# Result rows of single token tiles added one unit later, and six buffers for the experts' rows

## The reference, cut to what matters

```python
logits = xt @ Wr + br
top_p, top_idx = jax.lax.top_k(softmax(logits), 2)
weights = top_p / top_p.sum(axis=-1, keepdims=True)
xe = xn[None] * ln_g[:, None, :] + ln_b[:, None, :]            # per expert
h = gelu(einsum('end,edh->enh', xe, W1) + b1[:, None, :], approximate=False)
y = einsum('enh,ehd->end', h, W2) + b2[:, None, :]
out = (weights[:, :, None] * y_of_the_two_experts).sum(axis=1)
x = x + out
```

## Time and profile before

| | |
|---|---|
| median of 3 runs | 2281.2 us |
| the profiled execution | 2286.24 us |
| its span, first to last instruction | 2284.5 us |
| mean granted clock of TensorE | 0.953 |
| busy: PE, DVE, ACT, POOL | 89%, 50%, 27%, 46% |
| experts' units in the span | about 1850 to 2284.5 us |
| single tiles | about 2153 to 2284.5 us |

### The profile page before, as it was taken

How to read it: one execution, slowest core, us unless ns; L and a number is a source line. 1 busy time by engine, 2 the same in 40 slices (tenths; PEclk the granted TensorE clock), 3 DMA queues, 4 the chain that set the end, 5 groups by cost and what they waited for, 6 DMA issues and landing times.

```text
span 2284.5 us, 26178 instructions
## 1 busy us (share of the span) xinstructions
PE 2023.8 (89%) x8235; PEld 1382.6 (61%) x8235; DVE 1136.1 (50%) x2348; ACT 606.6 (27%) x1262; POOL 1051.0 (46%) x1049
## 2 busy tenths in 40 slices
PE   7999999979999999999776688889988679999987
PEld 3456446535555555555344456677777568888886
DVE  4999999324333434334566656545545831111111
ACT  2333323311111111112422231222222542222232
POOL 0000000066666666666566666666665124444343
PEclk9999999989999999999988899999999579999999
DMA  7432324345555655565644444333334374444463
GB/s 274 159 129 100 136 118 173 131 152 184 181 182 175 189 176 183 177 184 175 168 124 121 132 142 127 91 88 90 90 92 75 141 265 121 121 120 121 115 177 74
DMA packets 129381, 329.69 MB, mean 144 GB/s; under 512 B 24928, under 2 KB 57728, under 8 KB 127968
## 3 DMA queue, kind: packets, MB, share of 16 engines
q0 software_dynamic: 54672, 134.89, 23.7%
q1 hardware_dynamic: 71280, 191.33, 22.8%
q10 hardware_dynamic: 3296, 1.80, 0.3%
HBM read 199.22 MB, written 128.71 MB: 144 GB/s over the span
## 4 chain that ended last, share of the span: by engine, by line
PE 73%; DVE 9%; issue 6%; another core or an unknown queue 6%; DMA 3%; ACT 2%; POOL 1%; DVEq 0%; ACTq 0%; POOLq 0%
PE bank L576 26%; PE bank L637 14%; PE bank L1794 8%; PE bank L1805 7%; PE bank L1714 4%; PE bank L1723 4%; PE bank L512 3%; PE bank L1626 1%; DVE arena L662 1%; DMA work<-ffn_tokens,work 1%; DVE arena L363 1%; ACT arena L569 1%; DMA out<-xn,work 1%; PE bank L1652 1%
## 5 line engine op out<-in xcount | busy, mean ns | idle before, releaser
L576 PE MATMUL bank<-arena,work 128*128 128x512 f32 x1600 | 753.4, 604 | 42.4 <-ACT arena L569 23.7
L662 DVE TENSOR_TENSOR arena<-arena,bank 128x257 f32 x880 | 370.4, 421 | 616.5 <-PE bank L637 336.3
L637 PE MATMUL bank<-arena 128*128 128x257 f32 x1760 | 494.1, 394 | 86.8 <-DVE arena L662 50.5
L617 POOL DMA_INDIRECT arena<-table_bwd,arena x440 | 430.4, 978 | 231.9 <-issue 96.4
L617 POOL DMA_INDIRECT arena<-table_fwd,arena x440 | 425.2, 966 | 213.3 <-issue 97.3
L576 PEld LDWEIGHTS bank<-arena,work 128*128 128x128 f32 x1600 | 297.6, 192 | 318.3 <-issue 286.1
L637 PEld LDWEIGHTS bank<-arena 128*128 128x128 f32 x1760 | 331.5, 196 | 237.8 <-issue 198.2
L569 ACT ACTIVATE arena<-bank 128x512 f32<-128x512 f32 x400 | 238.9, 599 | 804.0 <-PE bank L576 577.2
L1794 PE MATMUL bank<-xn,arena 128*128 128x256 f32 (+1 forms) x1120 | 204.1, 341 | 0.0
L1547 ACT ACTIVATE arena<-bank,work 128x256 f32<-128x256 f32 (+1 forms) x280 | 120.9, 432 | 299.3 <-PE bank L1794 271.0
L860 POOL MEMSET arena<- 128x6425 f32 x1 | 5.5, 5454 | 423.4 <-PE bank L532 423.4
(11 more groups left out here) (316 smaller groups left out, 1634.7 us busy)
## 6 DMA issues: line engine op xcount, KB each, us to landing
table_fwd<-arena SPq DMA_DIRECT2D x100, 512.0 KB
table_bwd<-arena SPq DMA_DIRECT2D x100, 512.0 KB
arena<-in_W SPq DMA_DIRECT2D x35, 1024.0 KB
arena<-in_W SPq DMA_DIRECT2D x2, 4096.0 KB, 13.5
arena<-table_fwd,arena POOLq DMA_INDIRECT x440
arena<-table_bwd,arena POOLq DMA_INDIRECT x440
mix_rows<-arena SPq DMA_DIRECT2D x25, 256.0 KB
arena<-mix_rows SPq DMA_DIRECT2D x50, 128.0 KB
```

Of the source, the lines that this page charges most:

```text
L576: last = pe.matmul(ps[4 + s % 2][:, :], xT[t % 2][:, k * P:(k + 1) * P], ar(W_off[d] + k * 4096 + c * 512, 512), start=(k == 0), stop=(k = ...
L617: e.indirect_dma_start(msg[b][:, 0:C], None, table[d], bass.IndirectOffsetOnAxis(ap=idx[d][:, n % TE:n % TE + 1], axis=0)).then_inc(s_ga[b ...
L637: pe.matmul(ps[SEG[n % len(SEG)]][:, 0:W], oh[b], msg[b], start=True, stop=True).then_inc(s_sm, 1)
L662: vec.tensor_tensor(to, to, ps[SEG[n % len(SEG)]][:, 0:W], ALU.add).then_inc(s_ac, 1)
```

## The change

The list of buffers for `aux` grows from four to six; the two new ones lie where `gtmp` was, and the three columns `spare`, which ScalarE writes and nobody reads, move out of their way. In GpSimd's loop the scatters of single tiles are issued one step later: step u issues those of unit u-3 while these are pairs, step 24 issues none, and from step 25 on step u issues that of unit u-4. What is left is issued behind the loop.

```diff
-        spare = [work[:, 2900 + j:2901 + j] for j in range(3)]
+        spare = [work[:, 3000 + j:3001 + j] for j in range(3)]
...
-        AR = 4
-        aux = [work[:, 4 * C + j * AUX:4 * C + (j + 1) * AUX] for j in range(AR)]
+        AR = 6
+        aux = [work[:, o:o + AUX] for o in (*(4 * C + j * AUX for j in range(4)), 2436, 2436 + AUX)]
...
                 for u in range(UNITS):
                     unit_gather(u)
-                    if u >= 3:
+                    if 3 <= u < PAIRS + 3:
                         for t in tiles(u - 3):
                             add_rows(t)
-                for t in range(first(UNITS - 3), TX):
+                    if u > PAIRS + 3:
+                        add_rows(first(u - 4))
+                for t in range(first(UNITS - 4), TX):
                     add_rows(t)
                 e.wait_ge(s_sc, 16 * TX)
```

## The result

| | before | changed |
|---|---|---|
| median of 17 runs each | 2282.58 us | 2272.93 us |
| profiled execution | 2286.24 us | 2274.95 us |
| its span | 2284.5 us | 2273.2 us |

The ratio is 0.9959, 95% interval 0.9947 to 0.9970: 9.4 us less (6.8 to 12.1). The forecast was 6.5 us less. The changed kernel is faster by more than 0.2%, and the time lies within the stated range.

The account below looks back on a forecast made before the run. TensorE, busy 89%, was taken to stall on gathers queued behind scatters in GpSimd's queue. Nine turns at 7.24 us save 6.5 us, all other terms 0, so 2281.2 us becomes 2274.7 us; range 2272.3 to 2281.4 us.

Parts of the forecast that it names:

- What bounds the stage: Experts' single tiles: gathers queue behind scatters waiting for VectorE and get one turn; the chain takes 9.52 us against 7.24.
- The gain of the nine turns: TensorE's nine loop turns from 2183.65 to 2255.37 us: 71.72 us becomes 65.2 at 7.24 each, gain 6.5 us.
- How late gathers land: Single tiles' gathers land 5.2 to 6.4 us after issue; two turns, 14.5 us, then leave slack of 5.1 us or more.
- What stays at unit 24: Last pairs into singles: TensorE's 2.77 us idle and the slower-clock turn, 1.63 us over, stay; none of 4.4 us counted.
- Scatters don't move in time: Single tiles: scatters still start when VectorE releases them; only gathers move, one turn to the front.
- The end: Tail after TensorE's last product: unchanged, 0 us, with 11 us to the span's end; at most 4.35 us dearer.
- Four buffers would bring back the stall: Experts' rows: with four buffers, unit v's load waits for y_out of v-4 behind it, putting the next gather back at a turn.
- Smaller stalls outside the profile: Rival, single tiles: gathers land 1 to 2 us sooner in timed runs, gain some 2 us, 2279.2 us; chance 0.28.
- The clock behind the stalls: Rival, single tiles: three stalls each also cost 1.63 us of lower clock, gain 11.4 us, 2269.8 us; chance 0.06.
- Scatters as the period: Slower rival, single tiles: scatters wait for each other's landing, 6.07 or 6.8 us apart; at 8.7, 2287.8 us; chance 0.05.
- New wait: Rival, single tiles: earlier gathers still don't come through, turns stay at 7.97 us, gain 0 to 1, 2280.7 us; chance 0.04.
- The 2.3 us: Skill's fit for a 131 KB gather's landing: chain 5.3 us against 7.24, no stalls, change worth 0, 2281.2 us.

Follow-up runs that it names:

- e12: Kernel before, four buffers, with single tiles' scatters issued one unit sooner (unit u-2 instead of u-3): ratio 1.0405.
- e6: Kernel before without the W1 weight loads of units 24 to 34 (old weights used there), order and four buffers kept: ratio 0.9958.
- e1: Kernel before with six buffers for the experts' rows and `spare` moved, scatters in the old order: ratio 0.9987.
- e4: The changed kernel run once more, nothing altered, against the kernel before on the same chip: ratio 0.9954.
- e3: Changed kernel with unit 20's two scatters (tiles 40 and 41) also one unit later: ratio 0.9934 against the kernel before, 2099.76 us.
- e2: Kernel before with only the new scatter order, single tiles one unit later, and four buffers as before: ratio 0.9953, 2103.83 us.
- e5: The kernel before run once more, nothing altered, on the second chip: ratio 1.0003.
- e9: Kernel before, four buffers, with two more semaphores for the experts' rows that nobody uses: ratio 0.9995.
- e10: Kernel before, four buffers, without GpSimd's wait before the experts' rows for units 4 and 5: ratio 1.0003.
- e11: Kernel before, four buffers, two of them and `spare` moved to the columns that the change uses: ratio 0.9993.
- e8: Changed kernel, six buffers, with single tiles' scatters issued two units later (unit u-5): ratio 0.9973 against the kernel before.

## Why the prediction was right, and where its steps failed

- **What bounds the stage: right.** Gathers behind a scatter, one turn's length, a landing that exceeds it under the weights' load. e12 moves it the other way, e6 takes the load away; both answer as the chain of waits says.
- **The gain of the nine turns, 6.5 us: right for that profile, 6.49.** Forecast and result use the same 71.72 us of one execution; the other profiles in the old order give 4.0 to 7.9.
- **How late gathers land: partly wrong.** The 5.2 to 6.4 us were read from the chain that ended last, which holds late ones only. In e1 seven of ten landed after 2.9 to 4.3 us; in the new order (e4) some took up to 8.3. The landing at which a stall begins, 4.1 us, comes out right with e1's stalls, and the slack of a whole turn covers the error.
- **What stays at unit 24: right,** 2.79 us and a clock of 0.81 behind it. I took it as given; e3 shows it was the same fault one step earlier in the queue, worth 4 us.
- **Scatters don't move in time: right** (the earlier trace rows and the rows of after), and the end of the tiles with them.
- **The end, 0 us: wrong by 1.6.** The term was mis-sized: I counted only to the last scatter and held everything behind it fixed. GpSimd's last drain takes 5.04 us with four buffers and 3.1 to 3.2 with six. From TensorE's last product to the end of the span it is 9.6 us in the changed kernel and not the 11 forecast.
- **Four buffers would bring back the stall: wrong** (e2). I looked at what the load waits for and not at what the queue would be waiting for at that place anyway.
- **The rivals.** Smaller stalls outside the profile: in e5's execution they were (69.26 us where the profile before has 71.72), in the four on the faster chips not. The clock behind the stalls: it comes once in nine turns in four of the six profiles in the old order, and not in the other two. Scatters as the period: reached in e3, at 6.85 us on average, near the larger of its two figures, 6.8, and harmless, though from tile 42 on with only 0.1 us to spare. New wait: none. The 2.3 us that the prediction works out from the Trainium skill (DMA: Bandwidth & Descriptors, "Anatomy of one DMA — SWDGE (gpsimd) path") are seen nowhere: the quickest landing of a single tile's gather in e1, e4 and e12 is 2.7 us.
- **The whole:** the median, 2272.93, lies 0.6 us inside the fast end of the stated range. That is in part luck: the three runs that the forecast starts from had a median 1.4 us under that of all 17, and a range set out from the latter would have ended 0.8 us above the measured time. 6.5 + 1.6 = 8.1 us from the two profiles lies within the interval of 6.8 to 12.1. The middle of it, 9.4, is 1.3 above, and e2's 9.9 us (6.8 to 12.9) is about 3 over its profile's turns (72.1, the mean of e1 and e9 to e11, less 65.2). These remainders lie within the intervals, and no run settles whether they are anything.

## What to carry to other kernels

A DMA issued behind one that waits for a result has that result's time, not its own: write down for each place of an in-order queue what it waits for and how many turns are left until its data is needed, and put the one with the short deadline ahead. Before adding buffers for the new order, ask whether the queue wouldn't stand at that point anyway. A chain that ended last shows the late transfers only; read the others too before calling a landing typical. And look for the same fault at the seams between loop stages, where it was worth another 4.1 us beside the change's 9.7.

## What the runs showed of the hardware

- The same program takes 2111 to 2113 us on two chips and 2284 us on another. Its last stage is alike: from turn 24 on the changed order takes 65.23 + 27.59 us on a fast chip (e4) and 65.23 + 27.57 us on the slow one (e8). The difference lies earlier; in the stretch from 400 to 1200 us TensorE is busy 759 us on the one (e9) and 714 us on the other (e5), and the DMA engines move 188 and 170 GB/s. Times of these chips can't be compared, so each run is set against the kernel before on its own chip.
- A pause of TensorE of 2.0 to 2.4 us was followed by a lower granted clock in some cases (2.02, 2.22, 2.25, 2.40 us) and not in others (2.09, 2.18, 2.24, 2.30 us), at 1.6 us for such a turn. The ten pauses of 2.7 to 2.8 us at unit 24 were each followed by a slower turn, 8.6 to 8.9 us.
- A gather of 128 rows of 1 KB landed 2.8 to 4.1 us after its start where the DMA engines moved 84 GB/s (e12), and 2.7 to 8.3 us where they moved 172 (e4).
- GpSimd's final drain took 5.04 us in all eight profiles with four buffers and 3.08 to 3.17 us in all six with six.
